# Attention units of the first kind: the output task O1 between the input transposes X0 and X1, queries and keys one step later

## What is computed

```python
q = _split_heads(x @ Wq + bq); k = _split_heads(x @ Wk + bk); v = _split_heads(x @ Wv + bv)
scores = jnp.einsum('bhqd,bhkd->bhqk', q, k) * scale
sparsity = scores.max(axis=-1) - scores.mean(axis=-1)
_, top_idx = jax.lax.top_k(sparsity, U)
attn = jax.nn.softmax(scores_sel, axis=-1)          # of the chosen queries
out_sel = jnp.einsum('bhuk,bhkd->bhud', attn, v)
out = jnp.zeros_like(q).at[bi, hi, top_idx].set(out_sel)
return x + out @ Wo + bo                            # x is layer-normed before
```

## Time and profile before

| | us |
|---|---|
| median of 3 timed runs | 1687.62 (1687.0 to 1689.92) |
| profiled execution, its own time | 1682.62 |
| its span, first to last instruction | 1680.9 |
| TensorE busy | 1490.2 |
| VectorE busy | 1111.5 |
| ScalarE busy | 663.6 |
| GpSimd busy | 550.5 |

### The profile page before, as it was taken

How to read it: one execution, slowest core, us unless ns; L and a number is a source line. 1 busy time by engine, 2 the same in 40 slices (tenths; PEclk the granted TensorE clock), 3 DMA queues, 4 the chain that set the end, 5 groups by cost and what they waited for, 6 DMA issues and landing times.

```text
span 1680.9 us, 25260 instructions
## 1 busy us (share of the span) xinstructions
PE 1490.2 (89%) x8707; PEld 1057.1 (63%) x8756; DVE 1111.5 (66%) x2182; ACT 663.6 (39%) x924; POOL 550.5 (33%) x697
## 2 busy tenths in 40 slices
PE   4688998998898559999998899999999999999888
PEld 2333443343343148888877688878788787877676
DVE  3778778777877865555656858576674857575432
ACT  1176666666666512322233333323343332322211
POOL 5345534534632012513220323223322323233130
PEclk8599899999999969999999999999999999999997
DMA  5222312222222030011100100001010100101000
GB/s 150 50 46 66 69 42 66 65 50 58 52 59 52 2 129 26 26 51 38 33 26 13 38 1 22 18 1 37 0 37 0 37 0 12 25 0 26 4 10 13
DMA packets 56285, 60.99 MB, mean 36 GB/s; under 512 B 15637, under 2 KB 41509, under 8 KB 56221
## 3 DMA queue, kind: packets, MB, share of 16 engines
q1 hardware_dynamic: 42525, 43.85, 10.1%
q0 software_dynamic: 13408, 16.29, 4.5%
q10 hardware_dynamic: 288, 0.00, 0.0%
HBM read 25.48 MB, written 8.90 MB: 20 GB/s over the span
## 4 chain that ended last, share of the span: by engine, by line
PE 50%; issue 23%; DVE 12%; POOL 9%; ACT 5%; DMA 1%; POOLq 0%; DVEq 0%; another core or an unknown queue 0%; ACTq 0%; SPq 0%
PE ps L1730 12%; PE ps L1758 9%; PE ps L810 6%; PE ps L783 4%; PE ps L797 4%; PE ps L744 3%; POOL h L1358 3%; DVE mc L497 3%; PE ps L1741 2%; POOL kT L1336 2%; PE ps L752 2%; ACT pT0a L671 2%; PE ps L1770 1%; PE ps L1716 1%; DVE race L601 1%
## 5 line engine op out<-in xcount | busy, mean ns | idle before, releaser
L497 DVE TENSOR_REDUCE mc<-ps 128x2 f32<-128x1024 f32 x256 | 306.2, 1220 | 42.5 <-PE ps L783 42.3
L1758 PE MATMUL ps<-w_hi,h 128*128 128x256 f32 x1024 | 224.3, 302 | 0.3 <-DVE h L1578 0.3
L250 POOL DMA_DIRECT2D k_st<-k_hi x256 | 123.2, 487 | 259.4 <-PE ps L797 245.3
L1639 ACT ACTIVATE h<-ps 128x512 fp32r<-128x512 f32 x128 | 76.5, 598 | 328.9 <-PE ps L1791 202.9
L1730 PE MATMUL ps<-xT_b,w_hi 128*128 128x512 f32 x512 | 176.6, 427 | 5.7 <-ACT maskT L1633 5.7
L1358 POOL TENSOR_TENSOR h<-hf,h 128x512 fp32r<-128x512 f32 x64 | 82.8, 1294 | 301.9 <-DVE h L1589 301.9
L1758 PEld LDWEIGHTS ps<-w_hi,h 128*128 128x128 f32 x1024 | 168.1, 191 | 5.4 <-DVE h L1578 3.5
L1578 DVE SCALAR_TENSOR_TENSOR h<-ps,h 128x512 fp32r<-128x512 f32 x128 | 88.4, 691 | 124.1 <-ACT h L1639 122.8
L783 PE MATMUL ps<-k_st,q_st 48*128 48x512 f32 x512 | 138.4, 538 | 35.8 <-DVE mc L497 34.7
L783 PEld LDWEIGHTS ps<-k_st,q_st 48*128 48x128 f32 x512 | 52.2, 200 | 166.7 <-issue 82.0
L1758 PE MATMUL ps<-w_lo,h 128*128 128x256 f32 x512 | 143.9, 281 | 0.0
(11 more groups left out here) (261 smaller groups left out, 3391.9 us busy)
## 6 DMA issues: line engine op xcount, KB each, us to landing
q_st<-q_hi SPq DMA_DIRECT2D x256, 32.0 KB, 2.0
k_st<-k_hi POOLq DMA_DIRECT2D x256, 32.0 KB, 1.9
q_st<-q_lo SPq DMA_DIRECT2D x128, 32.0 KB, 2.1
k_st<-k_lo POOLq DMA_DIRECT2D x128, 32.0 KB, 1.9
x<-in_x_dram SPq DMA_DIRECT2D x8, 512.0 KB, 3.9
x_dram<-x SPq DMA_DIRECT2D x8, 512.0 KB, 2.9
yn<-x_dram SPq DMA_DIRECT2D x16, 256.0 KB, 4.5
x<-x_dram SPq DMA_DIRECT2D x16, 256.0 KB, 3.8
```

What stands on the lines that cost most here:

```text
L250: eng.dma_start((q_st, k_st)[which][par][64 * e + DH * r:64 * e + DH * r + DH, j, :].bitcast(F32), src[(2 * j + e) * DH:(2 * j + e + 1) * ...
L497: v.tensor_reduce(mc[par][:, qt, 2 * HU + j:MC:NPAIR], ps[:, at:at + 2, :], AX_X, ALU.max).then_inc(max_done, 1)
L1639: a.activation(h[s][m % 2][0][:, :], ps[:, RING[s] + m % 2, :], ACT.Relu).then_inc(F[s]["relu"], 1)
L1758: last = t_.matmul(ps[:, ACC[s] + t // 2, (t % 2) * D:(t % 2 + 1) * D], h[s][m % 2][a][:, t * P:(t + 1) * P], ws[k][:, m, :], start=m == 0 ...
```

## The change

In the table for units of the first kind, O1 moves from step 4 to step 1, X1 from 1 to 2, Q from 2 to 3, K from 3 to 4. Nothing else is edited; the other kind's table stays as it is.

```diff
-TASKS = [[("V", 0, "E"), ("X0", 0, "L"), ("X1", 1, "E"), ("Q", 2, "E"), ("K", 3, "E"), ("O1", 4, "E"),
+TASKS = [[("V", 0, "E"), ("X0", 0, "L"), ("O1", 1, "E"), ("X1", 2, "E"), ("Q", 3, "E"), ("K", 4, "E"),
           ("mx", 5, "L"), ("mean", 6, "E"), ("O0", 7, "E")],
```

## The result

| | before | changed |
|---|---|---|
| median of 4 timed runs | 1688.77 us (1687.0 to 1690.0) | 1716.84 us (1715.84 to 1718.65) |
| profiled execution, its own time | 1682.62 us | 1717.41 us |

The ratio is 1.0172 with a 95% interval of 1.0148 to 1.0197: slower by 28.1 us. The forecast was 1720.5, slower. The two profiled executions lie further apart, 34.8 us.

The account below looks back on a forecast made before the run. TensorE, busy 89% of the span, holds half the chain; the keys' late transfer decides the change. Wait 20.3 + clock 14 - 1.4 for unit 4's fall = +32.9 on the median 1687.6 gives 1720.5 us, range 1702 to 1733.

Parts of the forecast that it names:

- The margin of the keys: Attention stage, even units: keys' pair 0 lands 0.3 us or less before scores k = 11 first read it.
- Steps 1 to 4: Even units of the changed kernel: these steps take 3.9, 3.5, 3.9 and 3.9 us, 1.1 us sooner than before.
- K free to k = 11: Step 5 of even units: the keys' transfer needs 4.8 us from K's freeing of misc to the scores.
- The wait's price: Step 5 of units 0, 2, ..., 12: scores wait for the keys' transfer, 2.9 us a unit, 20.3 us in seven.
- The clock's price: Even units: TensorE's clock falls in the longer wait of step 5, 2.0 us a unit, 14 us in seven.
- The other falls: Unit 4's low stretch in step 4 merges into the new fall, -1.4 us; falls behind odd units' step 3 stay.
- The base: Whole kernel: the increment of +32.9 us is put on the median 1687.6, not on the profiled execution of 1682.62.
- (a): Rival for step 5's wait: the wait comes but the clock costs little; 1698 to 1707 us, chance 0.18.
- (b): Rival for the attention stage: the clock costs most, each fall lasting as in unit 3; 1730 us, chance 0.17.
- (c): Rival for step 5: the keys' transfer is hidden and VectorE's chain alone counts; 1688 us, chance 0.03.
- (d): Rival, faster: the 1.1 us found up to step 5 is kept; 8 us less, 1680 us, chance 0.02.
- The price by the Trainium skill: Low clock in the attention stage: time times one less the clock's share, 3.2 us a unit, some 8 us more, 1728.

Follow-up runs that it names:

- e2: Kernel before with only O1 moved to step 3 and K to step 4, X1 and Q staying in place; 1710.29 us, ratio 1.0129.
- e5: Changed kernel with three of the six transfers of the keys' pair 0 issued on SP's queue instead of GpSimd's; 1705.76 us, ratio 1.0103.
- e6: Kernel before, task table unchanged, GpSimd issuing the keys of pair 1 ahead of pair 0 in units 0, 2, ..., 12; 1707.51 us, ratio 1.0106.
- e12: Changed kernel with the x_in load moved later and unread matmuls added, 16 in step 5, 6 in odd units' step 3; 1693.14 us, ratio 1.0024.
- e9: Kernel before with the unread matmuls of e7 and the x_in load moved behind the keys' second half; 1671.38 us, ratio 0.9915.
- e4: Changed kernel with 16 unread matmuls ahead of scores k = 11 in step 5 of units 0, 2, ..., 12; 1705.88 us, ratio 1.0093.
- e1: Kernel before, unchanged, run again for a second profile; 1686.02 us.
- e11: Changed kernel, unchanged, run once more; 1716.36 us, ratio 1.0189.
- e7: Kernel before with unread matmuls, 6 in odd units' step 3 and 4 in step 4 of units 0, 2, ..., 12; 1680.07 us, ratio 0.9953.

## Why the prediction held, step by step

- **The margin of the keys.** Right. The forecast read from the earlier trace rows that k = 11 had 0.3 us or nothing to spare. e2 (K late, tasks otherwise in order), e5 (transfer shorter) and e6 (transfer later, no task moved) all move the time the way that this asks.
- **Steps 1 to 4.** Forecast 3.9, 3.5, 3.9, 3.9; measured 3.87, 3.52, 3.91, 3.90. O1's place does save VectorE's and ScalarE's time early, and VectorE's chain behind K takes it back in step 5.
- **K free to k = 11.** Forecast 4.8 us, measured 4.9 in unit 12.
- **The wait's price.** Forecast 20.3; e12 against e9 gives 20.8 by the profiles, 21.8 by the medians, 18.4 by the ratios.
- **The clock's price.** Forecast 14 us in seven falls at 2.0. The size held: the seven steps 5 of the changed kernel's profile take 12.8 us more than those of e12, where the clock stays up in them. Unit 12 fits: 524.84 - 519.62 = 5.2 us from k = 11 to the next exponential for 3.2 in unit 8, 2.0 more. Taken off by the fill of e4, it gave back 11 us by the medians (1716.8 to 1705.9), 13 by the ratios.
- **The other falls.** The forecast took 1.4 off for unit 4 and left the odd units' falls as they are. That step was not right, and that it did no harm in the first pair of profiles is luck. The falls behind step 3 are gone from units 3, 7, 9 and 11, one has come in unit 13, and units 3 and 7 have the waits behind q_st<-m_rows instead, which cost 4.1 us each in steps 6 and 7, wait and clock, and 1.2 in the next step 0; the odd units together differ by 0.5 us. In the even units unit 0 lost a fall of before as unit 4 did, and unit 2 got one in step 1, 1.5 us. Falls of the clock are not a sum of terms that stay in place; each moves the units' beat and with it the others.
- **The base.** The increment was put on the median of before, +32.9. The first pair of profiled executions differs by 34.8 us, the second (e1 and e11) by 1716.26 - 1686.02 = 30.2, the medians by 28.1. In all four profiles unit 15 and what follows take 1125 us, so the differences lie in the attention stage. Held against e9, before loses 12.4 us there to low stretches and to the waits behind q_st<-m_rows in its first profile, and 16.9 in its second; held against e12 without its 1.2 us, the changed kernel loses 25.9 and 24.4. So the clock's term, forecast as 14 - 1.4 = 12.6, is 13.5 in the first pair and 7.5 in the second, and about 8 by the medians (28.1 less the wait's 20.3). This term was the mis-sized one: what before itself loses was read from an execution 5 us faster than the median and was taken to stay, all but 1.4 us. The 3.4 us that the forecast gave as what a measurement can tell came from three runs; 25 runs of before lie 22 us apart.
- **The rivals.** (a), the clock costs little, and (b), it costs most, were both possible; measured lies between (a)'s upper end and the forecast. (c) and (d) fell by the row of k = 11, which names the transfer, and by the time. The price by the Trainium skill (TensorE: Matmul & The Clock Gate, section Terms) would have been some 8 us above the sum, further off: the low stretches cost less than half their length, as in the earlier trace rows. In unit 12 a fall with 6.8 us at the lower clock cost 2.0.

## What to carry to other kernels

A task's place in a hand-written order is not only its own time and that of its neighbours: ask who reads what it makes and by how much the result is ahead. Here the busy engines gave nothing away, and the one row that decided was a wait of 0.8 us for a DMA in one unit of seven. And a price read from one execution holds what the clock did in that one: two profiles of before differed by 4.5 us in this stage alone. Last, read a wait of TensorE with two prices, the wait and the clock after it; work that nobody reads, put into the wait, took the second off for 0.5% in the kernel before and, with a load moved out of a small transfer's way, 0.85%.

## What the runs showed of the hardware

- Waits of TensorE of 1.3 to 1.9 us lowered its granted clock in some units and not in others of the same program, and in other units in the next execution; waits of 4.5 to 5.1 us (the changed kernel, e11) and of 3.4 to 4.1 us (e5) did in all seven units. With the waits filled two low stretches were left in the stage (e7); with the load moved too, none (e9) and one of 3.4 us (e12).
- One program's times spread over 1678.4 to 1700.3 us in 25 runs, the kernel with the waits filled over 1675.7 to 1683.9 in 10 runs of the same set (e7).
- Transfers of 16 KB issued 0.7 us behind a load of 512 KB on another queue were waited for until 5.3 us after the first issue (208.00 to 213.28, the changed kernel), and 5.1 to 5.3 us with the same 0.7 us in e1, e7 and e11. Where the load was issued 1.7 to 1.8 us ahead (e2) the wait was 0.3 and 0.5 us, and with 2.2 us or more (unit 5 of the changed kernel, units 3 and 7 of before) there was none.
